# Two rebuilt output projections, a split first load for the experts, and combination gathers issued three chunks ahead

## The chip, the cores and the metric

One core of a Trainium2 chip (trn2) runs the whole program. The metric is device time in microseconds (us). The engines are PE (TensorE; PEld is its weight load), DVE (VectorE), ACT (ScalarE), POOL (GpSimd) and SP (SyncE, which here only issues transfers).

## The reference, cut to what matters

Four blocks run on x of shape (2, 2048, 256), each followed by a residual sum and a layer norm. All data is float32.

```python
x = layernorm(x + attn0(x))      # causal, 16 heads of 16, 4 key/value groups; ctx @ wo.T
x = layernorm(x + moe(x))        # top 2 of 8 experts, capacity int(1.2*2*2048/8) = 614 slots per batch row and expert
x = layernorm(x + attn1(x))      # latent k/v, rope, mask by pages of 64; ctx @ wo
x = layernorm(x + ffn(x))        # two layers of windowed attention and a gated unit
# moe: logits = x @ router_w + b; p, idx = softmax(top2(logits)); expert: silu((t@w_fc+b)*(t@w_gate+b)) @ w_proj + b
#      out = sum_k p_k * expert_out[idx_k, slot_k]
```

## The kernel before

Stages follow each other with a barrier of all engines between them; tiles carry the stage's letter. A: projections of layer 0. B: attention of layer 0. C: its output projection, norm and router logits. D: routing. E: experts. F: combination of the experts' outputs, norm, and projections of layer 1. G: attention of layer 1. H: its output projection and norm (the same function as C, without the router). I, J, K twice: the last block. Tokens are handled in 8 chunks of 512 (NCK), each of 4 tiles of 128 (SUB). X is the activation, kept on chip.

**attention (L179).** An iteration covers 4 heads of one batch row, 8 iterations in all. At its end each head has left 16 rows of unnormalised context and one row of softmax sums in the DRAM scratch `ot`. POOL issues the loads of iteration i+1 during iteration i, so the last iteration has none.

**attention_output (L669), C and H.** SP loads the sums once (`sums`), DVE takes their reciprocal (`inv`), SP stores it in the DRAM scratch `inverse` and waits for the store. Then for each chunk SP loads the context rows (`num`) and, spread over the 16 rows of a head, the reciprocals (`den`); both have two slots. POOL multiplies them into `cx` (L747). PE multiplies `cx` by `wo` in 8 matmuls, each recorded as two instructions, into `pb` (L759). DVE adds X (`y`), takes the statistics (`st`, `mv`), waits for ACT's square root (`sd`), and writes the norm (`xn`, L829). ACT copies `xn` to X and, in H, issues four stores to `xp`. In C, PE also turns `xn` (L768), ACT copies it (`xnT`), and PE forms the logits (L774). PE's matmuls of chunk n+1 wait until `mv` of chunk n is written, because `pb` and `y` have one slot:

```python
            def body(n, b, pair, u):
                pe.wait_ge(c_ready, n + 3)
                pe.wait_ge(var_done, n + 1)
```

In C the activation X itself (4 MB) is loaded by POOL at the stage's start, and PE and DVE wait for it.

**experts (L981), E.** POOL issues the loads of expert 0's weights, then 64 scatters of 128 rows each (first the 32 of batch row 0, then the 32 of batch row 1) into `ein`, waits for all, and issues expert 0's row loads (`xin`). An expert has 1,228 rows, the first 614 from batch row 0, in 3 chunks of 384, 384 and 460 rows. PE turns a chunk (`turn`, L1089), multiplies it with both input matrices (L1104), turns the next chunk, and multiplies with the output matrix (L1117). The weights are split in two parts by ACT and DVE before their first use. `every` runs pairs of experts in a loop of 3 and the last pair behind it.

**combine_and_project (L1232), F.** POOL gathers 8 tiles per chunk (L1282). Chunks 0 and 1 are gathered up front; those of chunk n+2 stand two at a time before each of POOL's four subtractions `low(n, j)` (L1290), which wait for ACT. DVE runs `combine(n+1)` (L1412 to L1430), then `products` and `rotated` of chunk n (L1438 to L1446); PE waits with `turn(n+1)` (L1309) for the combined rows, and with `latent(n)` (L1316) for the turned ones. POOL first sets `eps` and the 2,048 columns of `v`.

Of the kernel before, what the change touches and what calls it, by code (L numbers as in the profile page):

```python
# [178 lines left out]
def attention(nc, sem, tag, nk, page, qh, ql, kh, kl, vs, ident, ot, zeros):  # L179
# [93 lines left out]
    with ExitStack() as ctx:  # L273
# [27 lines left out]
        zeroed, zeros_out = sem(tag + "zeroed"), sem(tag + "zeros_out")  # L301
        o_done, o_out = sem(tag + "o_done"), [sem(f"{tag}o_out{i}") for i in range(2)]
# [30 lines left out]
        def _(pool):  # L333
# [37 lines left out]

# [48 lines left out]
        def _(sp):  # L420
# [33 lines left out]
            sp.wait_ge(zeros_out, 16 * len(zeros) + 1)  # L454
            for c in range(2):
# [213 lines left out]
def attention_output(nc, sem, tag, ot, woT, x_src, X, ident, router, xp, inverse):  # L669


    with ExitStack() as ctx:
        sb = lambda n, s, t: ctx.enter_context(nc.sbuf_tensor(tag + n, s, t))
        num = sb("num", [P, 2, KC, CH], F32)
        den = sb("den", [P, 2, KC, CH], F32)
# [4 lines left out]
        y = sb("y", [P, SUB, D], F32)  # L680
        xn = sb("xn", [P, SUB, D], F32)
        xnT = sb("xnT", [P, KC, CH], F32)
        st = sb("st", [P, SUB, 6], F32)
        mv = sb("mv", [P, SUB, 2], F32)
        sd = sb("sd", [P, SUB], F32)
        rs = sb("rs", [P, SUB], F32)
        eps = sb("eps", [P, 1], F32)
        idf = sb("idf", [P, P], F32)
        rw = sb("rw", [P, KC, E_], F32)
        rb = sb("rb", [P, E_], F32)  # L690
        pb = [ctx.enter_context(nc.psum_tensor(f"{tag}pb{i}", [P, CH], F32)) for i in range(5)]
        w_in, a_in = sem(tag + "w_in", 0), [sem(f"{tag}a_in{u}", 0) for u in range(2)]
        c_ready, mm_done = sem(tag + "c_ready"), sem(tag + "mm_done")
        var_done, sd_done, n_done = sem(tag + "var"), sem(tag + "sd"), sem(tag + "n_done")
        t_done, xt_done, lg_done = sem(tag + "t"), sem(tag + "xt"), sem(tag + "lg")
        x_copied, st_done, dch, fence = sem(tag + "xc"), sem(tag + "st"), sem(tag + "dch"), sem(tag + "fence")
        lg_kept = sem(tag + "lgk")
        eps_set, sums_in, inv_done, inv_out = sem(tag + "eps"), sem(tag + "si", 0), sem(tag + "id"), sem(tag + "io")
        sem.start()
        block = ctx.enter_context(nc.Block())  # L700
        wcount = 2 + (2 if router else 0) + (1 if x_src is not None else 0)

        def chunks(eng, body):
            with eng.Fori(0, B) as b:
                with eng.Fori(0, CPB // 2) as pair:
                    for u in range(2):
                        body(b * CPB + pair * 2 + u, b, pair, u)

        def skewed(eng, first, second, swapped=False):


            def both(n, *nxt):
                if swapped:
                    second(n)
                first(n + 1, *nxt)
                if not swapped:
                    second(n)

            last = CPB // 2 - 1
            first(0, 0, 0, 0)  # L720
            for b in range(B):
                with eng.Fori(0, last) as pair:
                    for u in range(2):
                        both(b * CPB + pair * 2 + u, b, pair + u, 1 - u)
                n = b * CPB + last * 2
                both(n, b, last, 1)
                if b < B - 1:
                    both(n + 1, b + 1, 0, 0)
            second(NT // SUB - 1)

        @block.gpsimd
        def _(pool):
            pool.dma_start(wo[:], woT.rearrange("(kc p) n -> p kc n", p=P)).then_inc(w_in, 16)
            pool.dma_start(idf[:], ident).then_inc(w_in, 16)
            pool.memset(eps[:], EPS).then_inc(eps_set, 1)
            if router:
                pool.dma_start(rw[:], router[0].rearrange("(kc p) n -> p kc n", p=P)).then_inc(w_in, 16)
                pool.dma_start(rb[:], router[1]).then_inc(w_in, 16)
            if x_src is not None:
                pool.dma_start(X[:], x_src.rearrange("(t p) c -> p t c", p=P)).then_inc(w_in, 16)  # L740

            pool.sem_inc(c_ready, 1)

            def body(n, b, pair, u):
                wait_apart(pool, a_in[u], b * (CPB // 2 * 64) + pair * 64 + 63, fence)
                wait_apart(pool, mm_done, n, fence)
                pool.tensor_tensor(cx[:, u], num[:, u], den[:, u], ALU.mult).then_inc(c_ready, 1)  # L747
            chunks(pool, body)

        @block.tensor  # L750
        def _(pe):
            pe.wait_ge(w_in, wcount * 16)

            def body(n, b, pair, u):
                pe.wait_ge(c_ready, n + 3)
                pe.wait_ge(var_done, n + 1)
                for s in range(SUB):
                    for c in range(KC):
                        last = pe.matmul(pb[s // 2][:, s % 2 * D:(s % 2 + 1) * D], cx[:, u, c, s * P:(s + 1) * P],  # L759
                                         wo[:, c], start=c == 0, stop=c == KC - 1)  # L760
                last.then_inc(mm_done, 1)

            def logits(n):
                if router:
# [1813 lines left out]
```

## Time and profile before

| | us |
|---|---|
| median of 3 runs (lowest, highest) | 4732.59 (4718.12, 4739.34) |
| the profiled execution, its own time | 4731.27 |
| its span, first to last instruction | 4729.8 |
| C, first load issued to last instruction | 989.91 to 1096.15 |
| E, first scatter to the first turned rows | 1128.22 to 1218.40 |
| F, first instruction to last store issued | 1939.05 to 2163.37 |
| H, first load issued to the next stage's first | 3112.78 to 3224.66 |

Times within the execution are counted from the span's start. "Busy" is the time in which an engine had an instruction in work; the granted clock (PEclk) is TensorE's, as a share of full speed, so 0.50 is its lower level of 1.2 GHz and 1.00 its upper of 2.4 GHz. Text in square brackets behind a row is the engine's idle time before it, and what ended it.

### The profile page before, as it was taken

The page shows a single profiled execution, that of the slowest core. Times are in us where ns is not written, and L with a number is a line of the kernel's source. Part 1 is how long each engine was busy: PE and PEld are TensorE (multiplying, and loading weights), DVE is VectorE, ACT ScalarE, POOL GpSimd, SP SyncE. Part 2 cuts the span into 40 slices and gives each one's busy share as a digit, 9 for nine tenths or more (in the row PEclk, how much of TensorE's full clock was granted, in tenths as well). Part 3 has the DMA queues.
Part 4 walks back from the last instruction along what each step waited for, and adds up shares of the span by engine and source line. Part 5 has one row for each costly group of instructions (what it writes and reads, how often), then busy time and mean ns, then how long its engine had stood idle before and what let it go on. Part 6 is the DMA issues. An engine that isn't in the chain of part 4 may idle for free. (4 is left out here: it accounts for less than half of the span.)

```text
span 4729.8 us, 80736 instructions
## 1 busy us (share of the span) xinstructions
PE 3988.1 (84%) x24868; PEld 2687.6 (57%) x24868; DVE 2983.5 (63%) x6105; ACT 2498.5 (53%) x4342; POOL 1582.1 (33%) x2150
## 2 busy tenths in 40 slices
PE   5999999962699999664999999957979798979798
PEld 2544444431699999432444444435767676767676
DVE  1888888822354454454887867827957544967656
ACT  1477777740354454221676767733556554546554
POOL 2223233214200000252122111116979402979700
PEclk8789999986899999886999978978989898989999
DMA  7322223132212111357033323134456312446511
GB/s 175 94 58 33 34 36 49 21 112 81 80 55 91 53 55 52 99 172 122 8 52 55 58 44 52 25 103 132 152 170 181 105 36 74 156 155 181 160 54 45
DMA packets 333304, 410.27 MB, mean 87 GB/s; under 512 B 41308, under 2 KB 242477, under 8 KB 330124
## 3 DMA queue, kind: packets, MB, share of 16 engines
q1 hardware_dynamic: 289868, 270.15, 18.1%
q0 software_dynamic: 38464, 131.41, 13.9%
q8 instruction: 187, 3.06, 0.3%
q10 hardware_dynamic: 4608, 4.20, 0.3%
q14 instruction: 177, 1.45, 0.1%
HBM read 248.58 MB, written 156.19 MB: 86 GB/s over the span
## 5 line engine op out<-in xcount | busy, mean ns | idle before, releaser
L606 DVE TENSOR_REDUCE G_mpart<-G_pm 128x1 f32<-128x512 f32 (+3 forms) x1024 | 618.2, 651 | 201.3 <-PE G_pm L495 193.8
L606 DVE TENSOR_REDUCE B_mpart<-B_pm 128x1 f32<-128x512 f32 (+3 forms) x1024 | 618.1, 651 | 163.5 <-PE B_pm L495 155.8
L585 ACT ACTIVATE G_p<-G_psc 128x1024 f32<-128x1024 f32 (+1 forms) x576 | 532.8, 977 | 149.5 <-PE G_psc L532 147.1
L585 ACT ACTIVATE B_p<-B_psc 128x1024 f32<-128x1024 f32 (+1 forms) x576 | 532.5, 977 | 134.0 <-PE B_psc L532 131.7
L495 PE MATMUL G_pm<-G_ks,G_qs 48*128 48x512 f32 (+3 forms) x1664 | 462.8, 421 | 99.0 <-DMA G_ks<-G_one 55.3
L495 PE MATMUL B_pm<-B_ks,B_qs 48*128 48x512 f32 (+3 forms) x1664 | 456.0, 413 | 73.7 <-DMA B_ks<-B_one 41.9
L495 PEld LDWEIGHTS G_pm<-G_ks,G_qs 48*128 48x128 f32 x1664 | 250.0, 209 | 419.5 <-DVE G_mpart L606 216.4
L1888 POOL TENSOR_SCALAR J_pr<-J_pr,J_rc 128x256 f32<-128x256 f32 x512 | 462.1, 923 | 70.3 <-DVE J_rc L2033 70.2
L495 PEld LDWEIGHTS B_pm<-B_ks,B_qs 48*128 48x128 f32 x1664 | 244.0, 202 | 387.1 <-DVE B_mpart L606 218.8
L510 PE MATMUL G_po<-G_p,G_v 128*32 128x512 f32 (+3 forms) x2560 | 322.3, 588 | 0.1
L510 PE MATMUL B_po<-B_p,B_v 128*32 128x512 f32 (+3 forms) x2560 | 311.2, 570 | 1.2 <-POOL B_p L357 1.1
L532 PE MATMUL G_psc<-G_qs,G_ks 50*128 50x512 f32 (+3 forms) x1280 | 302.6, 413 | 9.3 <-issue 6.9
L532 PE MATMUL B_psc<-B_qs,B_ks 50*128 50x512 f32 (+3 forms) x1280 | 294.6, 405 | 8.9 <-issue 6.3
L1151 ACT ACTIVATE E_hs<-E_pH,E_bf 128x384 f32<-128x384 f32 (+1 forms) x192 | 115.5, 602 | 346.7 <-PE E_pG L1104 346.4
L1104 PE MATMUL E_pH<-E_xT,E_wfg 128*128 128x384 f32 (+1 forms) x1152 | 252.5, 355 | 25.6 <-DVE E_wfg L1190 18.7
L1990 ACT ACTIVATE J_pr<-J_pr,J_nm 128x256 f32<-128x256 f32 x512 | 253.0, 497 | 16.2 <-DVE J_nm L2029 15.7
L1104 PE MATMUL E_pG<-E_xT,E_wfg 128*128 128x384 f32 (+1 forms) x1152 | 249.2, 352 | 0.0
L1117 PE MATMUL E_pO<-E_wp,E_a 128*128 128x256 f32 (+1 forms) x1920 | 234.6, 283 | 0.0
L1104 PEld LDWEIGHTS E_pH<-E_xT,E_wfg 128*128 128x128 f32 x1152 | 211.0, 191 | 36.5 <-issue 26.2
L1117 PEld LDWEIGHTS E_pO<-E_wp,E_a 128*128 128x128 f32 (+1 forms) x1920 | 230.0, 184 | 0.0
L1195 DVE SCALAR_TENSOR_TENSOR E_z<-E_pG,E_bg,E_hs 128x384 f32<-128x384 f32 (+1 forms) x192 | 123.6, 644 | 165.8 <-ACT E_hs L1151 164.7
L1734 POOL TENSOR_TENSOR I_t<-I_qn,I_R 128x512 f32<-128x512 f32 x128 | 224.3, 1772 | 0.7 <-POOL I_R L1725 0.7
(300 smaller groups left out, 7881.5 us busy)
## 6 DMA issues: line engine op xcount, KB each, us to landing
J_v<-lve SPq DMA_DIRECT2D x64, 520.0 KB, 4.0
J_k<-lkT SPq DMA_DIRECT2D x64, 512.0 KB, 5.3
lve<-I_v SPq DMA_DIRECT2D x64, 260.0 KB, 2.1
lqT<-I_tT SPq DMA_DIRECT2D x64, 256.0 KB, 2.4
lkT<-I_tT SPq DMA_DIRECT2D x64, 256.0 KB, 2.8
J_q<-lqT SPq DMA_DIRECT2D x64, 256.0 KB, 4.3
ein<-B_z SPq DMA_DIRECT2D x32, 307.0 KB
E_xin<-ein POOLq DMA_DIRECT2D x8, 1152.0 KB, 6.2
```

Of the source, the lines that this page charges most:

```text
L495: last = pe.matmul(t[:, n * w:(n + 1) * w], qs[s][rows, q // SUB, h // 2, q % SUB * P:(q % SUB + 1) * P], ks[s][rows, h // 2 % NA, first:f ...
L510: last = pe.matmul(po[VW * h:VW * (h + 1), off:CH], v[s][:, kb, h % nk], p[:, t % PSLOTS, h, at:at + CH - off], start=first[t], stop=final[t],
L532: score = pe.matmul(psc[:, h, at:at + CH - off], ks[s][rows, h // 2 % NA, kb * P:(kb + 1) * P], qs[s][rows, qc, h // 2, off:CH], start=Tru ...
L585: act.activation(p[:, t % PSLOTS, 2 * pr:2 * pr + 2, span(t)], psc[:, 2 * pr:2 * pr + 2, span(t)], ACT.Exp, scale=SC).then_inc(e_done[pr], 1)
L606: dve.tensor_reduce(mpart[:, heads[0] % 2, a:z, qb, kc], pm[slots[e]][:, 0:len(heads) * w].rearrange("p (h k) -> p h k", k=w), AX, ALU.max ...
L1104: last = pe.matmul(bank[ht % 2][:, 0:w], wfg_p[pw][:, i, kc, ht * P:(ht + 1) * P], xT[px][:, kc, 0:w], start=kc + j == 0, stop=kc == KC - ...
L1117: last = pe.matmul(pO[j // 2][0:r, j % 2 * D:(j % 2 + 1) * D], a[pa][:, ht, j * P:j * P + r], wp_p[pw][:, ht], start=j % 2 + ht + i == 0, ...
L1151: act.activation(hs[:, ht % 2, 0:w], pH[ht % 2][:, 0:w], ACT.Identity, bias=bf[:, s, ht:ht + 1]).then_inc(hs_done, 1)
L1195: dve.scalar_tensor_tensor(z[:, ht % 2, 0:w], pG[ht % 2][:, 0:w], bg[:, s, ht:ht + 1], hs[:, ht % 2, 0:w], ALU.add, ALU.mult).then_inc(z_d ...
L1734: last = pool.tensor_tensor(t2[:, u, :, :, a:a + H], qn[:, u, :, :, z:z + H], R[:, :, ds(w_, 1), a:a + H].to_broadcast([P, 2, LH, H]), ALU ...
L1888: last = pool.tensor_scalar(pr[:, u, pos(h)], pr[:, u, pos(h)], rc[:, u, pos(h):pos(h) + 1], None, ALU.mult)
L1990: last = act.activation(pr[:, u, pos(h)], pr[:, u, pos(h)], ACT.Exp, bias=nm[:, u, pos(h):pos(h) + 1], scale=8.0, accum_out=su[:, u, pos(h ...
```

## The change

1. attention: a new argument `preload`. In B, POOL issues the load of X at the start of the last iteration, and SP waits for it at the end. G passes none.
2. attention_output is rewritten. The reciprocals no longer go through DRAM: PE spreads `inv` over the heads' rows with two matmuls against a 0/1 matrix `pk` (`spread`, into `pB`), and DVE multiplies (`product`) in place of POOL. `num` has 4 slots, `y`, `mv` and the projection's banks `pX` two. ACT writes the norm straight to X (`norm`, scale `rs`, bias `nb`), and in H one store per chunk goes out from X. The logits are formed with the router's weights held and the rows streamed, into four groups of 32 partitions, and turned back. Every engine's order is written out over the 8 chunks.
3. experts: SP loads the first 384 rows of expert 0 when batch row 0's scatters have landed, and the rest when batch row 1's have. The first pair stands in front of the loop, and expert 0's input matrices are split before its first rows.
4. combine_and_project: three chunks are gathered up front and the gathers of chunk n+3 stand before `low(n, j)`; `eps` and `v` are set by DVE.

```diff
@@ attention: POOL's body, and SP's end
+                    if preload and t == 0 and static(i, NIT - 1):
+                        pool.dma_start(preload[0][:], preload[1].rearrange("(t p) c -> p t c", p=P)).then_inc(kept_in, 16)
...
+            if preload:
+                sp.wait_ge(kept_in, 16)
@@ attention_output, SP
             for b in range(B):
+                sp.dma_start(sums[b * half:(b + 1) * half], heads[b * NH:(b + 1) * NH].rearrange("g (q t) -> q g t", t=CH)
+                             ).then_inc(sums_in, 16)
+            sp.dma_start(pk[:].rearrange("p n c j -> p (n c j)"), pick).then_inc(pk_in, 16)
+            for n in range(NCK):
+                if n >= NSLOTS:
+                    sp.wait_ge(c_ready, n - NSLOTS + 2)
+                numerators(n)
@@ attention_output, PE
+            def spread(n):
+                if n >= 1:
+                    pe.wait_ge(c_ready, n + 1)
+                rows = slice(n // 2 * 2 * NH, (n // 2 + 1) * 2 * NH)
+                for c in range(KC):
+                    last = pe.matmul(pB[:, c], pk[rows, n % 2, c], inv[rows], start=True, stop=True)
+                last.then_inc(b_mm, 1)
...
+            def logits(n):
...
+                for c in range(KC):
                     for s in range(SUB):
+                        last = pe.matmul(pL[s * GROUP:(s + 1) * GROUP, 0:P], rw[:, c], xnT[:, c, s * P:(s + 1) * P],
+                                         start=c == 0, stop=c == KC - 1, skip_group_check=True)
...
+            for n in range(NCK + 3):
+                if n + 1 < NCK:
+                    spread(n + 1)
+                if router and 0 <= n - 3 < NCK:
+                    logits(n - 3)
+                if router and 0 <= n - 2 < NCK:
+                    turn(n - 2, 0)
+                if n < NCK:
+                    project(n)
+                if router and 0 <= n - 2 < NCK:
+                    turn(n - 2, 1)
+                if router and 0 <= n - 3 < NCK:
+                    turn_logits(n - 3)
@@ attention_output, DVE
+            for n in range(NCK + 4):
+                if router and 0 <= n - 4 < NCK:
+                    keep_logits(n - 4)
+                if 0 <= n - 1 < NCK:
+                    scales(n - 1)
+                if n + 1 < NCK:
+                    product(n + 1)
+                if n < NCK:
+                    statistics(n)
@@ attention_output, ACT: norm(n-1), logits_out(n-3), turned(n-2,0), store(n-1), turned(n-2,1), deviation(n)
@@ experts, POOL
-                                                oob_is_err=False).then_inc(sent, 16)
-            pool.wait_ge(sent, 16 * B * TOPK * (S // P))
-            load_rows(0, 0)
+                                                oob_is_err=False).then_inc(sent[b], 16)
+            for b in range(B):
+                pool.wait_ge(sent[b], 16 * TOPK * (S // P))
@@ experts, SP
+            for b in range(B):
+                sp.wait_ge(sent[b], 16 * TOPK * (S // P))
+                if b == 0:
+                    sp.dma_start(xin[:, 0, 0:early], ein[0:early * P, :].rearrange("(t p) c -> p t c", p=P)
+                                 ).then_inc(x_first, 16)
+            sp.dma_start(xin[:, 0, early:XT - 1], ein[early * P:(XT - 1) * P, :].rearrange("(t p) c -> p t c", p=P)
+                         ).then_inc(x_rest, 16)
+            sp.dma_start(xin[0:LAST, 0, XT - 1], ein[(XT - 1) * P:ROWS, :]).then_inc(x_rest, 16)
@@ combine_and_project, POOL and DVE
-            pool.memset(eps[:], EPS).then_inc(eps_set, 1)
-            pool.memset(v[:], 1.0).then_inc(eps_set, 1)
             gather(0, 0, PER)
             gather(1, 0, PER)
+            gather(2, 0, PER)
             for n in range(NCK):
                 for j in range(RJ):
-                    if n + 2 < NCK:
-                        gather(n + 2, j * PER // RJ, (j + 1) * PER // RJ)
+                    if n + 3 < NCK:
+                        gather(n + 3, j * PER // RJ, (j + 1) * PER // RJ)
                     low(n, j)
...
+            dve.memset(eps[:], EPS).then_inc(eps_set, 1)
+            dve.memset(v[:], 1.0).then_inc(eps_set, 1)
```

## Rows read from the trace of the kernel before

**Rows 1.** The page: busy time of each engine over the span.
```profile
PE 3988.1 (84%) x24868; PEld 2687.6 (57%) x24868; DVE 2983.5 (63%) x6105; ACT 2498.5 (53%) x4342; POOL 1582.1 (33%) x2150
```
**Rows 2.** Windows: stretch, its length, busy of each engine, clock, DMA share, GB/s.
```profile
990.00:1098.00 108.00, 62.87 (x320) 54.09 (x320) 44.33 (x129) 20.81 (x33) 23.12 (x14) 0.74 0.36 125
1042.00:1050.00 8.00, 6.82 (x46) 6.12 (x45) 5.54 (x17) 2.44 (x4) 2.73 (x2) 1.00 0.43 141
...
1228.00:1234.00 6.00, 6.00 (x36) 6.00 (x35) 2.31 (x4) 4.42 (x8) 0.00 (x0) 1.00 0.00 0
...
1939.00:2165.00 226.00, 136.14 (x352) 69.58 (x352) 122.07 (x264) 45.06 (x97) 110.16 (x98) 0.82 0.53 163
...
3164.00:3204.00 40.00, 26.65 (x64) 20.29 (x64) 19.20 (x57) 5.41 (x8) 9.27 (x4) 0.67 0.40 132
```
**Rows 3.** Timeline of stage C: start us, duration us, engine, instruction.
```profile
989.91 0.67 SPq L860 DMA_DIRECT2D C_sums<-ot  x1
...
993.26 3.35 DVE L805 RECIPROCAL C_inv<-C_sums 128x512 f32<-128x512 f32 x1 [48.83 <-DMA C_sums<-ot]
...
1017.85 6.36 PE L759 MATMUL C_pb<-C_wo,C_cx 128*128 128x256 f32 x16 [33.09 <-POOL C_cx L747]
...
1079.34 3.70 PE L759 MATMUL C_pb<-C_wo,C_cx 128*128 128x256 f32 x16
...
1095.96 0.19 DVE L839 TENSOR_TENSOR LG<-C_pb,C_rb 128x32 f32<-128x32 f32 x1 [6.72 <-PE C_pb L774]
```
**Rows 4.** Timeline of stage H and the next stage's first instruction.
```profile
3136.01 5.42 PE L759 MATMUL H_pb<-H_wo,H_cx 128*128 128x256 f32 x16 [28.04 <-POOL H_cx L747]
...
3164.24 6.65 PE L759 MATMUL H_pb<-H_wo,H_cx 128*128 128x256 f32 x16 [3.57 <-DVE H_mv L819]
...
3205.17 6.67 PE L759 MATMUL H_pb<-H_wo,H_cx 128*128 128x256 f32 x16 [3.58 <-DVE H_mv L819]
...
3224.66 0.35 SPq L1558 DMA_DIRECT2D I_w<-in_l_wqkv  x1
```
**Rows 5.** Timeline of stage E's opening: first and last of 64 scatters, first two turns.
```profile
1128.22 1.09 POOL L1045 DMA_INDIRECT ein<-X,slot_s  x1 [0.30 <-issue]
...
1209.21 0.98 POOL L1045 DMA_INDIRECT ein<-X,slot_s  x1 [0.30 <-issue]
1211.84 1.08 POOL L1036 DMA_DIRECT2D E_xin<-ein  x1 [1.66 <-DMA ein<-X,slot_s]
...
1218.40 1.52 PE L1089 MATMUL E_pT<-E_idf,E_xin 128*128 128x128 f32 x6 [105.91 <-DMA E_xin<-ein]
...
1243.87 0.82 PE L1089 MATMUL E_pT<-E_idf,E_xin 128*128 128x128 f32 x6
```
**Rows 6.** Timeline of stage F: PE's turns of chunks 1, 2 and 5; L1326.
```profile
1979.89 1.04 PE L1309 MATMUL F_pb<-F_idf,X 128*128 128x128 f32 x8
...
1995.71 1.88 PE L1326 MATMUL F_pb<-F_xnT,F_wqs 128*128 128x512 f32 x4
...
2005.23 1.57 PEld L1309 LDWEIGHTS F_pb<-F_idf,X 128*128 128x128 f32 x8 [8.47 <-DVE X L1430]
...
2081.58 1.97 PE L1309 MATMUL F_pb<-F_idf,X 128*128 128x128 f32 x8 [6.19 <-DVE X L1430]
```
**Rows 7.** Stage F: who waited (total, times, longest), and the gathers' ns (min/median/max).
```profile
DVE F_y L1412 <- DMA F_Y<-eout,slot_g: 69.2, 7, 21.5
...
L1282 POOL DMA_INDIRECT F_Y<-eout,slot_g x64: 999/1010/1407, 1941.1 to 2121.7; - x64
```
**Rows 8.** Prices: groups by line (busy us, mean ns), and G's column-group matmuls.
```profile
L2000 ACT ACTIVATE X<-J_xn 128x256 f32 (+1 forms) x64 | 25.8, 403 | 9.4 <-DVE J_xn L2044 9.4
...
L2356 DVE TENSOR_TENSOR K_y<-K_pO,X 128x1024 f32<-128x1024 f32 x16 | 19.4, 1215 | 17.0 <-PE K_pO L2207 17.0
...
L815 DVE BATCH_NORM_STATS2 C_st<-C_y 128x6 f32<-128x256 f32 x32 | 11.2, 414 | 0.3
...
3103.28 1.07 PE L510 MATMUL G_po<-G_p,G_v 128*32 128x512 f32 x8
```

More of the change, by code:

```diff
@@ L699, in attention_output @@
         sem.start()
         block = ctx.enter_context(nc.Block())
[L701 to L720, printed above, removed]
-            for b in range(B):
[L722 to L729, printed above, removed]
+        @block.sync
@@ new lines, in _, with columns, numerators @@
+        def _(sp):
+            def columns(n):
+                return slice(n % CPB * CH, (n % CPB + 1) * CH)
+            def numerators(n):
+                for m in range(KC):
+                    first = n // CPB * NH * VW + m * (NH * VW // KC)
+                    o = ot[first:first + NH * VW // KC, columns(n)].rearrange("(h r) t -> h r t", r=VW)
+                    sp.dma_start(num[:, n % NSLOTS, m], o[:, 0:HD]).then_inc(n_in[n % NSLOTS], 16)
+            heads = ot.rearrange("(g r) t -> g r t", r=VW)[:, HD]
+            half = P // B
+            for b in range(B):
+                sp.dma_start(sums[b * half:(b + 1) * half], heads[b * NH:(b + 1) * NH].rearrange("g (q t) -> q g t", t=CH)
[5 more added lines that the diff above has]
+                numerators(n)
+            if xp is not None:
+                sp.wait_ge(stored, 16 * NCK + 1)
@@ L742, in _ @@
[L742 to L748, printed above, removed]
+                pool.dma_start(idf[:], ident).then_inc(id_in, 16)
+                pool.memset(rw[:], 0.0).then_inc(rw_set, 1)
+                wait_apart(pool, rw_set, 1, fence)
@@ new lines, in store, with norm @@
+            def store(n):
+                row = n // CPB * PADS + n % CPB * CH + 1
+                act.wait_ge(n_done, n + 2)
+                act.dma_start(xp[row:row + CH, :].rearrange("(s p) c -> p s c", p=P), X[:, n * SUB:(n + 1) * SUB, :]
+                              ).then_inc(stored, 16)
+            def norm(n):
+                u = n % 2
+                act.wait_ge(nb_done, n + 2)
+                for s in range(SUB):
+                    last = act.activation(X[:, n * SUB + s], y[:, u, s], ACT.Identity, bias=nb[:, u, s:s + 1],
+                                          scale=rs[:, u, s:s + 1])
+                last.then_inc(n_done, 1)
@@ new lines, in _ @@
+            for n in range(NCK + 3):
+                if 0 <= n - 1 < NCK:
+                    norm(n - 1)
+                if router and 0 <= n - 3 < NCK:
+                    logits_out(n - 3)
+                if router and 0 <= n - 2 < NCK:
+                    turned(n - 2, 0)
+                if xp is not None and 0 <= n - 1 < NCK:
+                    store(n - 1)
+                if router and 0 <= n - 2 < NCK:
+                    turned(n - 2, 1)
+                if n < NCK:
+                    deviation(n)
@@ L845, in _ @@
[L845 to L866 removed]
+                link(dve.reciprocal(rs[:, u], sd[:, u]), rs_done, n + 2)
@@ L1061, in every, with two @@
         def every(eng, first, body):
-            def two(pair, last):
+            def two(pair, last=False):
                 for s in range(2):
@@ L1068, in every, with opening @@
             first(0, 0, 0)
-            with eng.Fori(0, E_ // 2 - 1) as pair:
-                two(pair, False)
+            two(0)
+            with eng.Fori(1, E_ // 2 - 1) as pair:
+                two(pair)
             two(E_ // 2 - 1, True)
+        def opening(pair, s):
+            return isinstance(pair, int) and pair == 0 and s == 0
         def number(pair, s, c):
@@ L1185, in body @@
                 e, w = pair * 2 + s, width(t, k)
-                if c == 0:
-                    for g in range(WG):
-                        cols = slice(g * WC, (g + 1) * WC)
-                        dve.wait_ge(whi_done, e * WG + g + 2)
-                        dve.tensor_tensor(wfg_p[1][:, :, :, cols], wfg[:, :, :, cols],
-                                          wfg_p[0][:, :, :, cols].bitcast(F32), ALU.subtract).then_inc(wlo_done, 1)
+                if c == 0 and not opening(pair, s):
+                    weights_lo(pair, s)
                 for ht in range(HT):
```

272 lines of the change are left out of this document (146 added, 126 removed).

## The prediction

> **What bounds the kernel now.** I read the page first: PE is the busiest engine of the whole [rows 1], but that share is an average, and each stage the change touches has its own limit. So I read next the windows by stage, then the timelines of C, H, the opening of E and F, and last the waits.
>
> C and H are not bound by an engine. In H four chunks take from 3164.24 to 3205.17, 10.23 us each, in which PE is busy 67% and DVE 48% [rows 2, 4]. The reader is to see the bracket behind each projection: PE sat idle 3.6 us until the statistics were written. Products, sum and statistics stand one behind the other, and the clock stays low: 0.67 over that stretch, and a projection takes 6.65 us there against 3.70 at the upper level in C [rows 2 to 4]. C fills the gap with turns and logits, is 85% busy on PE at a clock of 1.00, and takes (1079.34 - 1017.85) / 7 = 8.8 us per chunk with its slower start [rows 2, 3]. Before the first projection lie 27.9 us in C and 23.2 us in H [rows 3, 4], spent on sums, reciprocal and a trip through DRAM.
>
> E's opening is bound by POOL: 64 scatters in (1209.21 - 1128.22) / 63 = 1.286 us steps while PE, DVE and ACT stand still [rows 5]. PE's first turn is at 1218.40, the second at 1243.87.
>
> F is bound by a wait: DVE waited 69.2 us for gathers, 21.5 of it at the start, so 47.7 us over six chunks [rows 7]. PE's turns are (2081.58 - 2005.23) / 3 = 25.45 us apart, and before each the bracket shows PE idle until X [rows 6].
>
> **The change, part by part.**
>
> C and H, start. The sums come in two loads; the first row to the reciprocal is 993.26 - 989.91 = 3.35 us now, the second issue adds some 0.9. The reciprocal takes 3.35 [rows 3]. Then `spread(0)`: two matmuls of 512 columns, four instructions, 1.88 us at the upper level [rows 6], 3.5 at the lower, where PE stands after its idle time. `product(0)` is one 128x1024 operation like K_y's, 1.2 us [rows 8]. `spread(1)` stands before `project(0)` in PE's order: 3.5 again, then the first projection, 5.4 us in H as now and 6.0 in C, between the first one's 5.42 and 6.36 [rows 3, 4]. Sum for H: 3112.78 + 4.25 + 3.35 + 3.5 + 1.2 + 3.5 + 5.4 = 3134.0; for C: 989.91 + 15.8 + 6.0 = 1011.7. The load of `pk` (256 KB) and the first `num` lie under the reciprocal. The removed load of X frees the queues here.
>
> H, steady. PE needs 1.8 for a spread and 3.4 for a projection at the upper level, 5.2. DVE spends 19.20 / 3.91 = 4.9 us per chunk now [rows 2, 4]; the norm leaves it for ACT (4 x 0.41, priced by the equal-sized statistics), the product comes (1.2), and the new bias 0.2: 4.7. Its chain still waits for ACT's root and its own links, which I put at 0.7: 5.4 us, DVE being the bound. ACT has 4 x 0.40 for the norm [rows 8] and a store issue beside it, so it is covered; POOL has nothing left. Seven chunks: 37.8. The tail from the last projection's end (3205.17 + 6.67) to the next stage, 12.8 us [rows 4], keeps its chain. 3134.0 + 37.8 + 12.8 = 3184.6 against 3224.66: **40 us**. Bounds: 5.2 a chunk (PE only) and a warm start give 44, 6.2 a chunk gives 34.
>
> C, steady. PE also has nine turns (eight in 1.04 [rows 6]) and the logits. These are 16 instructions of 128 columns into four column groups. G's column-group row has 8 instructions of 512 columns in 1.07, which would make them 0.5; the turns' pace of 0.13 each would make them 2.1 [rows 6, 8]. I take 0.7, near G's row, which has the same layout. 1.8 + 1.2 + 0.7 + 3.4 = 7.1, and DVE's 5.4 lies beside it. The first chunks have less: 5.4 and 6.2, then five of 7.1: 47.1. ACT must turn a chunk's second half around between two PE steps, with about 0.2 us to spare by the durations above; if it is late, PE waits that much. Tail as now, 1096.15 - 1083.04 = 13.1 [rows 3]: 1011.7 + 47.1 + 13.1 = 1071.9 against 1096.15: **24 us**. Bounds 18 (logits at 2.1 for five chunks) and 30.
>
> E. Scatter 32 ends near 1169, so the first 384 rows are on chip before 1180. Chunk 0's 25.5 us from turn to next turn [rows 5], which includes splitting the input matrices, then end by 1206, all under the scatters. The rest is issued when the last scatter has landed, 1211.84 [rows 5]. It is less than the present load's 1.2 MB, but POOL now starts expert 1's rows and weights at that moment too, which before waited for expert 0's split, so I keep the present 6.6 us: second turn at 1218.4 instead of 1243.87, 25.5 less. Against it: PE has stood idle again and starts at 0.50. The first turn at the lower level took 1.52, the second at the upper 0.82, and the clock was back at 1.00 from 1228 on [rows 2, 5]. Some 6 us of matmuls at half speed lose 3. Rule and row together: the Trainium skill, "TensorE: Matmul & The Clock Gate", "Part 1: The HAM clock gate", says that low is the default and sustained activity lifts it, so the split opening pays the lower level twice; by the present order alone the sum would be 3 us better. Last, 25 scatters now run beside DVE. Gathers beside DVE in F took 1010 in the median and 1407 ns at most [rows 7]; at 0.04 each that is 1. **21.5 us**, bounds 14 (0.4 on each of 25 scatters, 10 in all, partly under the chunk) and 25.
>
> F. POOL's first gather comes up to 1.8 us earlier, DVE's memset lying in its idle time. Then gather 2 fills POOL's wait, and each later one has a whole chunk to land. What is late next? PE's own row of work: from chunk 1's turn at 1979.89, whose gathers were issued ahead already, to the end of L1326, 1995.71 + 1.88 = 1997.6, where the next turn could start, is 17.7 us [rows 6]. DVE per chunk is 25.45 less a mean wait of 47.7 / 6 = 7.95, at most 17.5; POOL 110.16 / 8 = 13.8 plus its issue gaps, near 16 [rows 2, 7]. So 17.7: the six periods from chunk 1's turn save 6 x (25.45 - 17.7) = 46.5, and 1.8 at the start: **48 us**. Bounds: 17.0 gives 53; 22.5 gives 20 (below).
>
> Attention B gets one 4 MB load at the start of its last iteration, on a queue that is free then. Its matmuls need small rows stored by SP, which could land later; 0 to 17 us, I take 0.5. The first pair of experts ahead of the loop moves no work; zero.
>
> Sum: 24 + 21.5 + 48 + 40 - 0.5 = 133. The profiled execution took 4731.27 (span 4729.8, 1.5 outside it); 4598.3. The median lies 1.3 above it: **4599 us**, 2.8% less.
>
> **The rivals.**
>
> A, transfers hold F. The same bytes in 17.7 instead of 25.45 us lift the DMA share from 0.53 [rows 2] to 0.76. For it: gathers and stores are small pieces. Against: the queues' share is only a mean, and gathers have slack now. If 0.60 were the ceiling, the period would be 22.5 and F would give 20: 4627.
>
> B, POOL's indirect transfers stand still while DVE works. DVE is busy about half of a chunk's time in E, so 25.5 us of chunk 0 would hold the scatters back about 12; the same in F puts POOL, at 16 a chunk, at about 20 us. E gives 10, F 34: 4624. For it: one gather took 1407 ns. Against: the median of 1010 in F, beside a DVE busy 54% of the stage [rows 2, 7]. The Trainium skill, "SBUF — State Buffer", "Who interferes with whom", names such a lock for DVE's two-port modes; by that rule the price would be this rival's, and the trace's median speaks against it here.
>
> C, the load of X delays B: one late row group stops PE for up to the load's length. 4 MB at the 163 GB/s of F is 26 us [rows 2]; at half of it, 4612.
>
> D, the other side: the clock stays at the lower level in the four rebuilt stretches. H holds 0.67 at 67% busy [rows 2]. All at 0.50: C per chunk 3.6 + 2.4 + 1.4 + 6.7 = 14.1, ending near 1120 (24 slower); H 10.3 a chunk, 5 faster; F's 17.7 us get some 11 us more of matmul time, 28.5 a period (18 slower); E gives nothing. Sum 37 slower: 4769. Linear between, it decides from a mean clock of about 0.61 down. Against: C at 85% busy held 1.00.
>
> **How the numbers follow.** Forecast 0.76, A 0.12, B 0.05, C 0.05, D 0.02. All but D are faster by over 0.5% (24 us), about what a measurement of this kernel can tell from no change. Faster 0.96, same 0.02, slower 0.02; I move 0.02 from faster to same for mishaps together. The range: best bounds 30 + 25 + 53 + 44 = 152 give 4580, widened to 4574 for a warm start that I did not price; the upper end takes in A and B with C's worst bound, 4636. The likeliest case's own range is 4580 to 4615.
>
> **What would show it.** C's projections 7.1 us apart, ended by no wait for statistics; H's 5.4 apart at a clock near 1.00; the second turn of E near 1218 with the first near 1177; no DVE wait for gathers behind the first, turns 17.7 apart; B's end unmoved. Wrong if PE in C waits for ACT's copies, if H's DVE waits for `num`, or if F's turns wait for something other than X.

## The result, and the profile after

The changed kernel takes 4666.43 us (median of 4 executions, 4632.51 to 4678.41) against 4735.35 (4718.12 to 4739.34, 4 executions) for the kernel before: ratio 0.9855, 95% interval 0.9814 to 0.9897. It is faster by some 69 us, half of the 133 forecast, and its median lies above the range. Three later sets put it at 0.9853, 0.9839 and 0.9852 of the kernel before (by their medians 78, 84 and 66 us). The profiled execution took 4663.87 us (span 4662.3), 67.5 less in the span.

The page, and windows of C, of three of its chunks, of F, of two of F's chunks and of H (columns as in [rows 1, 2]):

```profile
PE 4017.9 (86%) x24940; PEld 2686.6 (58%) x24940; DVE 2993.6 (64%) x6059; ACT 2511.6 (54%) x4393; POOL 1544.4 (33%) x2130
```

```profile
1001.39:1103.00 101.61, 73.86 (x360) 49.31 (x360) 40.58 (x105) 30.50 (x65) 2.78 (x6) 0.75 0.15 50
...
1058.11:1087.50 29.39, 24.50 (x133) 18.08 (x132) 12.62 (x38) 10.82 (x24) 0.00 (x0) 0.83 0.00 1
1940.00:2126.00 186.00, 132.13 (x352) 64.73 (x352) 138.22 (x265) 45.26 (x97) 110.27 (x96) 0.86 0.61 196
1980.65:1999.02 18.37, 15.32 (x46) 7.48 (x44) 17.36 (x34) 5.48 (x12) 12.97 (x11) 1.00 0.57 179
1999.02:2018.40 19.38, 16.90 (x44) 8.25 (x45) 17.62 (x34) 5.47 (x12) 14.70 (x13) 0.91 0.73 233
3122.00:3144.00 22.00, 22.00 (x80) 14.48 (x80) 18.07 (x48) 8.58 (x19) 0.00 (x0) 1.00 0.36 118
```

H looks as forecast in these 22 us: PE is busy all the time, at the upper level. C is not: three chunks take 29.39 us, PE is idle for 17% of them and the clock is at 0.83. The timelines say why. C and H, to be read against [rows 3, 4]:

```profile
1001.39 1.28 SPq L729 DMA_DIRECT2D C_sums<-ot  x2
...
1009.62 3.35 DVE L904 RECIPROCAL C_inv<-C_sums 128x512 f32<-128x512 f32 x1 [55.18 <-DMA C_sums<-ot]
...
1028.47 1.23 DVE L873 TENSOR_TENSOR C_y<-C_pX,X 128x1024 f32<-128x1024 f32 x1 [5.13 <-PE C_pX L767]
...
1077.68 1.23 DVE L873 TENSOR_TENSOR C_y<-C_pX,X 128x1024 f32<-128x1024 f32 x1 [4.70 <-PE C_pX L767]
...
1080.78 0.16 DVE L899 TENSOR_TENSOR LG<-C_pL,C_rb 128x32 f32<-128x32 f32 x1
...
1081.09 0.65 PE L785 MATMUL C_pL<-C_xnT,C_rw 128*32 128x128 f32 x16 [2.90 <-DVE LG L899]
...
1082.18 5.28 PE L767 MATMUL C_pX<-C_wo,C_cx 128*128 128x256 f32 x16
...
1087.50 1.22 DVE L873 TENSOR_TENSOR C_y<-C_pX,X 128x1024 f32<-128x1024 f32 x1 [5.89 <-PE C_pX L767]
```

```profile
3083.09 1.26 SPq L729 DMA_DIRECT2D H_sums<-ot  x2
...
3090.76 3.35 DVE L904 RECIPROCAL H_inv<-H_sums 128x512 f32<-128x512 f32 x1 [53.09 <-DMA H_sums<-ot]
...
3103.09 5.25 PE L767 MATMUL H_pX<-H_wo,H_cx 128*128 128x256 f32 x16
...
3161.43 0.34 SPq L1643 DMA_DIRECT2D I_w<-in_l_wqkv  x1
```

Two things are to be seen. The reciprocal comes 8.2 and 7.7 us behind the first issue, not 4.25. And in C, PE's logits wait 2.90 us for DVE's addition of the logits of the chunk before (`LG`), which stands in DVE's order behind y and all the statistics of the chunk that PE has just projected, three chunks further on; the projection waits behind them, and runs at the lower level (5.28 us).

E's opening [rows 5]: the first turn, the first chunk's projections, and what ACT waited for:

```profile
1179.78 0.39 SPq L1298 DMA_DIRECT2D E_xin<-ein  x1
...
1183.50 1.51 PE L1152 MATMUL E_pT<-E_idf,E_xin 128*128 128x128 f32 x6 [63.41 <-DMA E_xin<-ein]
...
1192.24 1.22 PE L1167 MATMUL E_pG<-E_xT,E_wfg 128*128 128x384 f32 x6
...
1207.89 0.58 ACT L1220 ACTIVATE E_hs<-E_pH,E_bf 128x384 f32<-128x384 f32 x1 [21.97 <-remote]
...
1218.60 0.98 POOL L1099 DMA_INDIRECT ein<-X,slot_s  x1 [0.30 <-issue]
...
1226.20 0.58 ACT L1220 ACTIVATE E_hs<-E_pH,E_bf 128x384 f32<-128x384 f32 x1 [17.21 <-remote]
...
1240.31 0.81 PE L1152 MATMUL E_pT<-E_idf,E_xin 128*128 128x128 f32 x6
```

ACT waits here for one semaphore, by which PE tells that a group of 12 matmuls is done. The first group ended at 1191.24 and the second at 1193.46 (the row of 1192.24); the semaphore's own records stand at 1207.87 and 1226.17, 16.6 and 32.7 us later ("remote" stands for a release that the view can put down to no instruction close by). By its records PE did the work, was idle behind it, and the news was late; the clock agrees, which stood at the lower level from 1198 to 1232. So chunk 0 was not hidden under the scatters, and the second turn came at 1240.31, 104.6 us behind the first scatter (115.65 before, 90.2 forecast).

F: the gathers, and the additions that follow (columns: ns min/median/max, first to last).

```profile
L1364 POOL DMA_INDIRECT F_Y<-eout,slot_g x64: 998/1010/1292, 1940.6 to 2071.2; - x64
L1497 DVE SCALAR_TENSOR_TENSOR F_y<-F_Y,prob,X x32: 468/472/1561, 1955.5 to 2087.0; 128x256 f32<-128x256 f32 x32
L1501 DVE SCALAR_TENSOR_TENSOR F_y<-F_Y,prob,F_y x32: 471/480/2047, 1957.2 to 2088.7; 128x256 f32<-128x256 f32 x32
...
  DVE F_y L1497: 13.4, 1
```

As forecast, DVE waits for gathers once, for the first (13.4 us). The chunks are (2094.24 - 1980.65) / 6 = 18.93 us, not 17.7.

### The profile page after: what moved, and what is told of

Its sections match the earlier page's. It is cut to its first block and busy times, and to the rows that moved or that the text cites. A ratio compares the mean times of both kernels' runs of the same rounds, so it can differ in the third digit from the quotient of the medians.

```text
span 4662.3 us, 80358 instructions
## 1 busy us (share of the span) xinstructions
PE 4017.9 (86%) x24940; PEld 2686.6 (58%) x24940; DVE 2993.6 (64%) x6059; ACT 2511.6 (54%) x4393; POOL 1544.4 (33%) x2130
## 5 line engine op out<-in xcount | busy, mean ns | idle before, releaser
L1271 DVE SCALAR_TENSOR_TENSOR E_z<-E_pG,E_bg,E_hs 128x384 f32<-128x384 f32 (+1 forms) x192 | 123.7, 644 | 209.3 <-ACT E_hs L1220 186.3
```

What stands on the lines that cost most here:

```text
L1271: dve.scalar_tensor_tensor(z[:, ht % 2, 0:w], pG[ht % 2][:, 0:w], bg[:, s, ht:ht + 1], hs[:, ht % 2, 0:w], ALU.add, ALU.mult).then_inc(z_d ...
```

## The experiments

All are timed beside the kernel before on the same chip. Lengths of stages run from the first to the last instruction that writes one of the stage's own tiles; what H writes to X at its end (2 us in the changed kernel, 3 in the kernel before) is not in them. The changed kernel's are C 100.6, E 802.5, F 184.7, H 68.6 in its first trace; the kernel before's 105.4, 809.4, 223.4, 104.3.

**One part alone** (three kernels: the functions of one part from the changed kernel, the rest from the kernel before), and the changed kernel again.

> The kernel before with only the load of X moved into B and both output projections rebuilt. If the forecast's steps hold, C gives 24 us and H 40 us: 64 us, 1.35%. By the trace of the changed kernel it is C 5 and H 36, less 2 to 3 in the gap behind H: 38 us, 0.8%. If the moved load of X really holds up B (10.9 us longer in the changed kernel's trace), B is about 908 us long here too and the gain is 28 us; if that was only the clock, B is near 897.

> The kernel before with only the experts' split first load. By the forecast E is 21.5 us shorter (0.45%). In the changed kernel's trace the semaphore that tells ACT of PE's first projections came 16.6 us behind their recorded end, and the stage gained 7 us (0.15%). If that lateness belongs to this opening, it stands here again and the gain is 5 to 10 us; if it was an accident of one execution, the second turn follows at 1218 us and the gain is 20 us.

> The kernel before with only the gathers three chunks ahead and the two memsets on DVE. By the forecast F is 48 us shorter (1.0%), by the changed kernel's trace 39 us (0.8%).

> The changed kernel once more. If B and G were longer in its first trace (10.9 and 7.5 us) because of the change, they are so again; if because of the clock, their lengths go with their time at the lower level. If the late semaphore in E's opening belongs to the kernel, it is there again, and the times lie near 4666; if it comes and goes, the times lie in two groups some 25 us apart.

| kernel | ratio to before | 95% interval | its stages |
|---|---|---|---|
| outputs alone | 0.9916 | 0.9887 to 0.9945 | C 98.2, H 70.0, B 886.1 |
| experts alone | 0.9994 | 0.9970 to 1.0018 | E 802.4 |
| gathers alone | 0.9920 | 0.9892 to 0.9947 | F 185.0 |
| changed kernel again | 0.9853 | 0.9816 to 0.9891 | C 99.9, E 802.4, F 184.9, H 70.0 |

The parts add up to 39.7 + 2.8 + 37.8 = 80 us; the whole gave 70 by its ratio (interval 52 to 87) and 78 by the medians, so no part hinders another by anything that shows. Every stage that the change touches repeats its length to 2.5 us. The late semaphores stand again in both kernels with the new opening, by 16 to 17 us for the first. The other two kernels of this set, on the same chip, have the old opening, where PE starts behind the last scatter: there the first semaphores follow their groups within 0.02 us.

The load of X: B took 908.4 us in the first trace of the changed kernel and 897.4 before. Over all 20 traces B's length is 842.4 us plus 0.32 times its time at the lower clock level, within 1.2 us, with the load and without: before 897.4 with 170.7 low, experts alone 912.3 with 216.2, changed 908.4 with 208.8, changed again 881.1 with 119.7. So no cost of the load is seen in B; where the clock stood during B was luck.

**What holds back the semaphore in E.** Three kernels: batch row 1's scatters left out; the same replaced by plain stores; the first rows loaded late.

```diff
-            for b in range(B):          # half_scatters: 32 scatters instead of 64
+            for b in range(1):
...
+                        if b == 1:      # plain_stores
+                            row = (k * (S // P) + q) * P
+                            pool.dma_start(eout[row:row + P, :], X[:, b * (S // P) + q]).then_inc(sent[b], 16)
+                            continue
...
             for b in range(B):          # rows_late
                 sp.wait_ge(sent[b], 16 * TOPK * (S // P))
-                if b == 0:
-                    sp.dma_start(xin[:, 0, 0:early], ...).then_inc(x_first, 16)
+            sp.dma_start(xin[:, 0, 0:early], ...).then_inc(x_first, 16)
```

> The changed kernel with the 32 scatters of batch row 1 left out, and the waits for them with them: batch row 1's rows are missing from the result, and POOL is idle while PE works on expert 0's first chunk. If the scatters beside it are what holds back PE's semaphore (16.6 us behind the recorded end of the first group, and 17 to 18 us again for the second), the first two updates follow their groups within 0.2 us and the second turn comes 22 to 25 us behind the first, not 57. If something in the new order itself holds it back (the first pair written out ahead of the loop, the split input matrices ahead of the rows), the 57 us stand.

> The changed kernel with batch row 1's 32 scatters replaced by 32 plain stores of the same 128 rows each from POOL, to a scratch that is written over later: batch row 1's rows are missing from the result. If DMA traffic or POOL's issuing as such holds back PE's semaphore, it is late by 15 us or more again; if only indirect transfers do, the second turn follows the first by 22 to 30 us.

> The changed kernel with the load of expert 0's first rows issued behind the last scatter, as the rest is: only the early splitting of the input matrices is left of the overlap. If the scatters beside PE's work are the cause, no semaphore is late here, the first turn comes some 5 us behind the last scatter's landing and the second 22 us later: second turn at 1248 on the first trace's scale, against 1240 with the overlap and 1218 as forecast, so that the overlap is still worth 8 us. If the lateness is in the new order itself, the second turn comes 57 us behind the first and the stage is 30 us longer.

The semaphores are prompt in all three (within 0.02 us of the groups' ends), and the second turn follows the first by 23.6, 22.8 and 23.6 us; E takes 768.4, 766.8 and 809.4 us (in all 4652.88, 4602.41 and 4657.96, one execution each, against 4748.83). By themselves these look like a proof that the scatters are to blame. They are not one, because the next kernel of the same set has all the scatters beside PE's work:

```diff
+            sp.wait_ge(sums_in, 16 * B)             # sums first
             sp.dma_start(pk[:]..., pick).then_inc(pk_in, 16)
...
-                link(dve.tensor_tensor(y[:, u], ..., ALU.add), y_done, n + 2)
+                dve.tensor_tensor(y[:, u], ..., ALU.add).then_inc(y_done, 1)
+                if router and n >= 3:
+                    keep_logits(n - 3)              # logits early
+                dve.wait_ge(y_done, n + 2)
```

> The changed kernel with two edits in both output projections: SP issues the 0/1 matrix and the context rows only when the sums have landed, and DVE adds a chunk's logits right behind the sum y, ahead of the statistics. If the transfers queued behind the sums cost the 8.2 us from first issue to reciprocal, it falls to 4 to 4.5 in C and in H. If C's chunks of 8.1 to 9.8 us come from PE's wait for the logits' addition (2.9 us) and from the clock that falls in these waits, they go to 7.1 to 7.5 us and C is 12 to 16 us shorter than its 100 us; if PE's own row of work sets them, they stay over 8.

Its semaphores are prompt too, E takes 791.8 us, and the second turn comes 91.9 us behind the first scatter, right behind the load of the rest. In C the reciprocal comes 6.64 us behind the issue and in H 6.25 (7.36 to 8.64 and 6.75 to 8.01 in the 13 traces with the two loads and SP's order as it was), so that SP's order is a small part of it, and the four middle chunks take 6.96 to 7.17 us: C 89.6. The total was 4616.92 against 4748.83 in one execution.

Four more kernels took this apart:

> The changed kernel with one of the last kernel's two edits, in both output projections: the 0/1 matrix and the context rows are issued when the sums have landed. C: 1 us shorter at the start, chunks of 8 to 9.8 us as in the changed kernel. The opening of E has the same instructions on every engine as the changed kernel's, where PE's first two semaphores came 17 and 33 us late in three executions, but was prompt in the last kernel. If SP's longer stream in C made the difference, it is prompt here; if DVE's order did, they are late.

> The changed kernel with the other edit: DVE adds a chunk's logits right behind the sum y. If PE's wait for them sets C's chunks, these are 7.1 us and C is some 10 us shorter than 100, as with both edits. E's opening: prompt if DVE's order made the difference, late if SP's stream did.

> The changed kernel with one more instruction in E: SP waits for the identity matrix to have landed (it has, long before) ahead of its waits for the scatters. If the late semaphores hang on where things stand in SP's stream, they are gone and E is 10 us shorter; if they are tied to anything in PE's, ACT's or POOL's work in E, they stand.

```diff
             early = chunks[0][1]
+            sp.wait_ge(c_in, 16)                    # e4
...
-                pool.tensor_tensor(lo[:, n % 2, j], r[:, j], hi[...], ALU.subtract).then_inc(lo_done, 1)   # f1
+                dve.tensor_tensor(lo[:, n % 2, j], r[:, j], hi[...], ALU.subtract).then_inc(lo_done, 1)
```

> The changed kernel with F's 32 subtractions L1372 moved from POOL to DVE, each one step behind. In the changed kernel's trace DVE's additions F_r and F_y took up to 2.15 us where POOL's subtraction ran beside them (0.68 and 0.48 otherwise): 3.0 us per chunk, DVE being busy 93% of F's steady part. If the two cannot run side by side, every F_r and F_y takes its short time here and the four subtractions cost DVE 2.7 us, so that the chunks stay at 18.5 to 19 us. If the long ones had another cause (gathers, stores), they stay long, and the chunks take 21.6 us.

All four have prompt semaphores (E 790.8 to 792.2 us); they took 4619.98, 4636.69, 4626.07 and 4638.28 us in one execution each, against 4724.15. The last is, up to F, instruction for instruction the changed kernel. So neither theory of the expectations holds, SP's stream nor DVE's order: what differs between late and prompt is not in the kernel.

C: with the sums first alone it takes 98.2 us and its last chunks 8.1 to 9.8; with the logits early alone 90.3 us. Here are two chunks of that:

```profile
1050.12 0.65 PE L785 MATMUL C_pL<-C_xnT,C_rw 128*32 128x128 f32 x16
...
1051.18 3.62 PE L767 MATMUL C_pX<-C_wo,C_cx 128*128 128x256 f32 x16
...
1054.84 1.22 DVE L873 TENSOR_TENSOR C_y<-C_pX,X 128x1024 f32<-128x1024 f32 x1 [1.98 <-PE C_pX L767]
...
1056.31 0.65 PE L785 MATMUL C_pL<-C_xnT,C_rw 128*32 128x128 f32 x16 [0.96 <-DVE LG L902]
...
1057.38 3.62 PE L767 MATMUL C_pX<-C_wo,C_cx 128*128 128x256 f32 x16
...
1061.04 1.23 DVE L873 TENSOR_TENSOR C_y<-C_pX,X 128x1024 f32<-128x1024 f32 x1 [2.26 <-PE C_pX L767]
```

The projections are back at 3.62 us, the upper level, and the stretches at the lower level between C's chunks went from four to one; shown is that the place of one 0.16 us instruction on DVE costs C 10 us.

F, the additions `F_r` and the subtractions `F_lo`, in the changed kernel and with the subtractions on DVE:

```profile
L1531 DVE TENSOR_TENSOR F_r<-F_t x32: 675/926/2153, 1982.7 to 2121.1; 128x512 f32<-128x512 f32 x32
...
L1372 POOL TENSOR_TENSOR F_lo<-F_r,F_hi x32: 1257/1270/1446, 1984.3 to 2123.3; 128x512 fp32r<-128x512 f32 x32
```

```profile
L1525 DVE TENSOR_TENSOR F_r<-F_t x32: 683/686/718, 1950.0 to 2088.3; 128x512 f32<-128x512 f32 x32
...
L1532 DVE TENSOR_TENSOR F_lo<-F_r,F_hi x32: 680/683/693, 1952.1 to 2089.7; 128x512 fp32r<-128x512 f32 x32
```

Beside POOL's subtraction an `F_r` took up to 2.15 us; without it all 32 take 0.68 to 0.72. Of the 24 additions `F_r` and `F_y` that overlap a subtraction 23 are long, and they end 0.3 to 0.6 us behind POOL's, which keeps its 1.27 us; ten of them had begun 0.3 to 0.5 us before it, so who begins first does not decide here who waits. In the Trainium skill, "SBUF — State Buffer", "Who interferes with whom", a DVE instruction with two inputs in SBUF contends with a GpSimd instruction that reads SBUF; this trace agrees. The chunks stay at (2061.01 - 1947.87) / 6 = 18.86 us, so this isn't yet what sets them.

**The causes mended, and controls beside them.** In the first kernel the sums come in one load; the matrix's rows are reordered to fit:

```diff
-            for b in range(B):
-                sp.dma_start(sums[b * half:(b + 1) * half],
-                             heads[b * NH:(b + 1) * NH].rearrange("g (q t) -> q g t", t=CH)).then_inc(sums_in, 16)
+            sp.dma_start(sums[:], heads.rearrange("g (q t) -> g q t", t=CH)).then_inc(sums_in, 16)
...
+            # F, on ACT: the norm, as in C and H
+                    last = act.activation(X[:, n * SUB + s], y[:, s], ACT.Identity, bias=nb[...], scale=rs[...])
```

> The changed kernel with four edits. C and H: the sums come in one load of 128 rows, as in the kernel before, with the 0/1 matrix reordered to fit; if the two loads of 64 rows in steps of four cost the lateness, the reciprocal comes 3.3 to 4 us behind the issue in C and H instead of 7.7. C: the logits are added right behind y (10 us, as measured with that edit). F: the subtractions are on DVE, and ACT writes the norm to X as in C and H. DVE is then left with 4 x 0.41 less and 0.2 more per chunk, 17.4 us; if DVE is what sets F's 18.9 us per chunk, they go to 17.4 to 17.8, as I had forecast for the bound by PE, and F is 7 to 9 us shorter; if something else does, they stay. Sum: C 14, H 4, F 8: some 26 us faster than the changed kernel.

> The changed kernel as it is, on this chip. If the late semaphores go with the chip, they stand in every kernel of this set that has the overlap or in none.

> The changed kernel with the first rows loaded behind the last scatter, as once before. Beside s2 it gives the worth of the overlap: 17 us if s2's semaphores are prompt (E 809 against 792), 7 us if they are late (against 802).

> The changed kernel without batch row 1's scatters, whose rows are missing from the result. It tells something where s2's semaphores are late: late here too, then the scatters have no part in it; prompt, then they have.

The mended kernel: 4626.42 us, ratio 0.9798 (0.9768 to 0.9829), C 83.7, H 62.7, F 186.3. Against the changed kernel beside it (100.6, 69.0 and 182.4 us) that is 16.9 and 6.3 us shorter in C and H and 3.9 longer in F; of the 26 us expected the medians show 8, and that lies inside both intervals. The start of C in it:

```profile
974.22 0.67 SPq L727 DMA_DIRECT2D C_sums<-ot  x1
...
977.60 3.35 DVE L904 RECIPROCAL C_inv<-C_sums 128x512 f32<-128x512 f32 x1 [49.14 <-DMA C_sums<-ot]
```

The reciprocal comes 3.38 us behind the issue in C and 3.23 in H. The slow landing was the form of the two loads, whose outermost dimension has 4 entries (q). In the trace with the sums first, their 128 packets of 84 ns each start at up to 23 per 0.5 us, 4 at a time, and take 4.7 us in all; in the kernel before up to 79 start, some 15 at a time, and all take 1.5 us, in the mended kernel 1.6. The Trainium skill, "DMA: Bandwidth & Descriptors", "Why a DMA increments its semaphore by 16 and not by 1", has the rule: the slowest dimension decides how many of the 16 engines a transfer uses; the trace agrees. It would have warned me of this term, though it has no time for it.

F got no shorter (chunks of 19.3 us, 18.9 in the changed kernel beside it), though DVE's busy share fell from 93% to 79%: my theory that DVE's load sets F's chunks fell. The kernel moved a wait too: PE now waits for X until ACT has written it, 0.6 us in each of the six chunks, where it waited 0.7 for DVE in every second one; and the clock fell in four of the six chunks, not in three.

Beside it, the changed kernel took 4634.52 us (0.9839), with prompt semaphores: E 792.1, its second turn 92.5 us behind the first scatter. With the rows late it took 4645.67 (0.9850), E 809.5: the overlap is worth 17.4 us of E where the semaphores are prompt (the medians show 11 of it, inside the intervals). Without the second half of the scatters: 4618.9 in one execution, E 769.4, prompt; with a prompt control it tells nothing of late ones.

The changed kernel's opening with prompt semaphores, to be read against the rows of 1183.50 to 1240.31 above:

```profile
1163.80 1.51 PE L1152 MATMUL E_pT<-E_idf,E_xin 128*128 128x128 f32 x6 [63.29 <-DMA E_xin<-ein]
...
1171.57 0.58 ACT L1220 ACTIVATE E_hs<-E_pH,E_bf 128x384 f32<-128x384 f32 x1 [5.36 <-PE E_pG L1167]
...
1173.83 0.58 ACT L1220 ACTIVATE E_hs<-E_pH,E_bf 128x384 f32<-128x384 f32 x1 [1.16 <-PE E_pG L1167]
...
1208.64 1.54 PE L1152 MATMUL E_pT<-E_idf,E_xin 128*128 128x128 f32 x6 [21.37 <-DMA E_xin<-ein]
```

**The last set.**

> The changed kernel with only the edits in the output projections: one load of the sums, logits added right behind y. C near 84 and H near 63 us, against 100.5 and 69: 23 us faster than the changed kernel beside it, 0.5%, and some 2.2% faster than the kernel before.

> The changed kernel as it is, on the same chip, near 4640 to 4660. Its second turn in E comes 57 us behind the first if the semaphores are late, 45 us if they are prompt, and t1 shows the same.

| kernel | us | ratio (interval) | C | H | E | second turn behind the first |
|---|---|---|---|---|---|---|
| outputs mended | 4645.15 | 0.9831 (0.9792 to 0.9870) | 85.4 | 64.8 | 801.5 | 56.5, late |
| changed kernel | 4653.02 | 0.9852 (0.9812 to 0.9893) | 100.6 | 69.6 | 802.5 | 57.5, late |

Both are late, on another chip than the sets before. Twelve traces have the whole opening, all scatters and early rows. The 5 of the first trace, the first set and the last set are late; the 7 of the three sets between are prompt. Each set ran on one chip, and no set has both. The lateness is not confined to the executions whose traces were kept: by a straight line through time and mean clock, the 4 executions of the changed kernel beside the mended one lie 10 us below the 16 of the sets with late semaphores (scatter 3 us), while the kernel before differs by at most 2 us between those chips. C and H shorten as expected (by 15.2 and 4.8 us); by the medians the gain on the changed kernel is 8 us and lies inside both intervals, since one kernel's own times spread by some 40 us with the clock: the mended stages are shown, the total of 23 us is not.

## Why the prediction was wrong

The mechanisms of all four parts happened. Four terms of the sum were too large, and two of them hid a wait or a form that the diff shows.

**C, 24 us forecast, 4.7 measured** (989.91 to 1096.15 against 1001.39 to 1102.96). The step "the second issue adds some 0.9" failed: it priced the two loads by their issue, and their form made them land 4 us later. To the first projection's end it took 27.1 us, not 21.8; the other 1.3 are spreads of 3.75 us for 3.5, a projection of 6.4 for 6.0, and small waits between them. The step "1.8 + 1.2 + 0.7 + 3.4 = 7.1" was right for PE's work (6.96 to 7.17 with the logits early) and wrong as a period: it named no wait, and the bank of the logits has one slot, so PE's logits wait for an addition that DVE's order puts behind the statistics. Chunks took 6.7 to 9.8, 59.0 us in all for 47.1. The clock fell for 3.4 us in each of four chunks, which made part of it: with the logits early one such stretch was left. The tail took 15.5 for 13.1. I had looked for such a wait at ACT's copies and not at DVE's addition.

**E, 21.5 forecast, 6.9 measured in the first trace, 17.3 with prompt semaphores.** The step "chunk 0's 25.5 us end by 1206, all under the scatters" is right in the prompt traces; the 64 scatters took 85.1 us beside PE's work and 82.0 before, 3 us where I had put 1. The second turn came 23.2 us earlier. What is lost behind it, 6 us, is 1.9 in chunk 1, and 4.3 at the changes from expert to expert: from an expert's first turn to its second it takes 33.3 to 34.8 us, where before three of seven took 32.0. At all seven changes TensorE's clock now falls to the lower level for a while, in the kernel before at four, and the three without it are those of 32.0 us. Where it falls, PE's first group takes 3.3 to 4.2 us for 2.4. The late semaphores, another 10 us, could not be seen in the trace of before.

**F, 48 forecast, 38.7 measured.** The step "17.7 apart" took PE's own row of work at the upper level, as it stood in one chunk (with 2.4 us of waiting for ACT's `F_xnT` in it, which every chunk still has). The windows show it: 18.37 at a clock of 1.00, of which 0.66 is a wait for X, then 19.38 at 0.91, in turn. The 1.2 us a chunk are that wait in every second chunk and 1.7 us for the lower level in the others; this is an account from the trace, and no run took either away by itself. The 1.8 at the start did not come (the first turn stands 24.6 us behind the stage's first instruction, 24.7 before).

**H, 40 forecast, 33.5 measured.** The start took 25.3 us for 21.2, 3.4 of it the late sums. Seven chunks took 39.9 for 37.8: the first 6.4 us (DVE waited 1.7 for ACT's root), the second 7.4 (a projection of 5.1, with the clock at the lower level for part of it), four 5.56, and the last 3.8, for it has no spread behind it. The tail took 13.2 for 12.8. The step "DVE being the bound" failed: PE sets the steady period. Its work, put at 5.2, takes 5.56, and DVE waits 0.47 us for it in each, so that 5.4 came out near by luck.

**B.** The 0.5 for the load is below what can be seen (1.2 us), and rival C is out.

The sum: 133 less 19.3, 14.6, 9.3 and 6.5 is 83.3. B and G were 10.9 and 7.5 us longer in this trace than in that of before, at more time on the lower level, the last block 4.2 shorter; that gives 69, and the spans differ by 67.5. Rivals A and B did not happen: the DMA share rose to 0.57 and 0.73 in two chunks of F, near the 0.76 feared, and no turn waited for gathers behind the first; the scatters beside DVE's work went from 1.28 to 1.33 us apiece. Rival D happened in a small way, in C's waits.

**What stays open.** What makes PE's semaphores late in E's opening. The same kernel is late on some chips and prompt on another, so it goes with the chip or with something set up with it. It takes the new opening too: on a chip where this was late twice, the two kernels with the old opening were prompt. That the scatters beside PE's work are what it needs is likely and not shown, for the kernels with the rows late or with fewer scatters never ran on such a chip.

## What to carry to other kernels

Where a change reorders an engine's work by hand, list for each tile with one slot who frees it and what stands in front of that instruction on its engine: a 0.16 us addition behind 3 us of statistics cost 10 us. Price a load by its outermost dimension too: 4 rows outside made 256 KB land 4 to 5 us later. And before explaining a stage that got longer, set its length against its time at each clock level over several traces.

## What the runs showed of the hardware

- Stage B is longer by 0.32 us per us at the lower clock level, and that time varies by chance: between 119.7 and 235.4 us low, 881.1 to 918.3 us long, whatever the kernel. One kernel's times go with the mean clock in the same way (the first four executions of the changed kernel: 4632.51 at a mean clock of 0.910, 4663.87 at 0.901, 4669.0 at 0.899, 4678.41 at 0.896).
- In the sets of some chips PE's first two semaphore updates came 16.4 to 17.4 and 32.7 to 33.5 us late while POOL's scatters ran; in the others never. The traces of the late ones also hold fewer semaphore records (39,144 to 39,185 in three traces of the changed kernel, against 40,489 in the prompt one). Nearly all that are missing belong to E's scatters and to F, where POOL's indirect transfers run; outside E and F the numbers agree to one. They are missing in the two kernels with the old opening on such a chip as well, whose opening was prompt. In F only the record is missing: ACT's `F_xnT` started 0.04 us behind PE's turn, whose update has no record near it. In E the update itself was late, for ACT started with it. Whether the recording takes part in that can't be told from these runs.
- DVE's additions from SBUF took up to 2.15 us instead of 0.68 beside a POOL subtraction, whose own median was 1.27 (1.45 at most), even where the addition had begun 0.3 us before it.
